# B times delta u by token on GpSimd, in four more states of a selective scan

## The reference

```python
# u: (b, 128, 256), four directions k; delta = softplus(...); A = -exp(A_logs); 16 states n
def step(h, inp):
    dt, bt, ct, ut = inp
    h = exp(dt[..., None] * A) * h + (dt * ut)[..., None] * bt[:, None, :]
    return (h, einsum('bdn,bn->bd', h, ct))
ys = vmap(_selective_scan)(xs, delta, A, Bst, Cst, Ds)      # k = 0..3
y = ys.sum(0); y = (y * silu(z)) @ out_proj_w
```

## Time and profile before

| what | us |
|---|---|
| median of three runs | 206.13 |
| profiled execution | 204.65 |
| its span | 202.9 |
| scans, first start to end of the last | 20.55 to 115.2 |
| busy in the span: PE, DVE, ACT, POOL | 191.7, 156.7, 140.0, 96.3 |
| granted TensorE clock | 1.000 |

### The profile page before, as it was taken

One profiled execution on the slowest core, in us unless ns is written; L12 is line 12 of the kernel. 1 busy time (PEld: TensorE's weight loads), 2 busy tenths in 40 slices (PEclk: granted clock), 3 DMA queues, 4 the chain that ended last, 5 costly groups with the idle time before them and its releaser, 6 DMA issues.

```text
span 202.9 us, 2710 instructions
## 1 busy us (share of the span) xinstructions
PE 191.7 (94%) x784; PEld 88.0 (43%) x784; DVE 156.7 (77%) x264; ACT 140.0 (69%) x292; POOL 96.3 (47%) x117
## 2 busy tenths in 40 slices
PE   7799999799999978999999999989999999999992
PEld 2334654344545434455355457664323333333331
DVE  6386899999999999999999864857376664663843
ACT  3529896999999999989999814547836255253431
POOL 7575668698899859998899700000000000000000
PEclk9999999999999999999999999999999999999999
DMA  4799554438967679793956000000000000000000
GB/s 133 158 240 167 139 183 110 145 131 205 231 235 197 177 205 270 220 222 132 304 221 218 15 0 0 3 0 0 0 3 0 2 2 0 0 3 0 0 0 26
DMA packets 17661, 21.79 MB, mean 107 GB/s; under 512 B 7721, under 2 KB 9198, under 8 KB 17646
## 3 DMA queue, kind: packets, MB, share of 16 engines
q1 hardware_dynamic: 17470, 21.52, 38.1%
q10 hardware_dynamic: 176, 0.10, 0.2%
HBM read 21.35 MB, written 0.26 MB: 107 GB/s over the span
## 4 chain that ended last, share of the span: by engine, by line
PE 48%; DMA 12%; DVE 8%; POOL 6%; issue 5%; SPq 0%; DVEq 0%; ACT 0%; POOLq 0%
PE ps L1177 20%; PE ps L1192 11%; DMA cr<-c_rows 9%; PE ps L965 8%; POOL rings L411 6%; DVE rings L692 4%; DMA c_rows<-cb 3%; PE ps L972 2%; PE ps L888 1%; DVE ps L682 1%; PE ps L1199 1%; PE ps L1133 1%; PE ps L1152 1%; PE ps L1053 1%; PE ps L1104 1%
## 5 line engine op out<-in xcount | busy, mean ns | idle before, releaser
L411 POOL TENSOR_TENSOR rings<-rings,cr 128x512 f32<-128x512 f32 x59 | 73.3, 1275 | 10.3 <-DVE rings L692 4.7
L692 DVE TENSOR_TENSOR_SCAN rings<-rings,ps 128x512 f32<-128x512 f32 x64 | 74.4, 1203 | 0.8 <-ACT rings L502 0.4
L859 DVE TENSOR_TENSOR rings<-ps,si 128x512 f32<-128x512 f32 (+1 forms) x44 | 30.4, 691 | 25.3 <-ACT si L584 24.4
L584 ACT ACTIVATE si<-ps 128x512 f32<-128x512 f32 (+1 forms) x44 | 26.3, 597 | 32.7 <-PE ps L1177 32.5
L502 ACT ACTIVATE rings<-delta,a_neg 128x510 f32<-128x510 f32 x64 | 43.5, 707 | 0.1
L1177 PE MATMUL ps<-fd,wup 64*128 64x512 f32 (+1 forms) x176 | 41.5, 607 | 0.6 <-DVE fd L794 0.5
L483 ACT ACTIVATE scaled<-du_tok,b_tok 128x128 f32<-128x128 f32 x116 | 36.7, 387 | 0.4 <-PE ps L972 0.3
L965 PE MATMUL ps<-rings,ident 128*128 128x512 f32 x64 | 33.1, 598 | 1.9 <-POOL rings L411 1.9
L965 PE MATMUL ps<-rings,flip 128*128 128x512 f32 x64 | 32.3, 598 | 0.4 <-POOL rings L411 0.4
L1177 PEld LDWEIGHTS ps<-fd,wup 64*128 64x128 f32 (+1 forms) x176 | 15.9, 182 | 24.5 <-issue 14.1
L682 DVE TENSOR_TENSOR ps<-ps,du 128x512 f32<-128x512 f32 x35 | 23.5, 679 | 1.6 <-PE ps L991 1.0
(11 more groups left out here) (211 smaller groups left out, 171.9 us busy)
## 6 DMA issues: line engine op xcount, KB each, us to landing
cr<-c_rows SPq DMA_DIRECT2D x60, 256.0 KB, 3.9
wup<-w_up_dram SPq DMA_DIRECT2D x8, 341.0 KB, 5.8
wdn<-w_down_dram SPq DMA_DIRECT2D x4, 160.0 KB
wdn<-w_down_dram SPq DMA_DIRECT2D x4, 128.0 KB
w_conv<-conv_w_dram SPq DMA_DIRECT2D x1, 384.0 KB, 5.5
xc<-x_chan_dram SPq DMA_DIRECT2D x2, 128.0 KB, 4.7
w_conv<-conv_w_dram SPq DMA_DIRECT2D x1, 192.0 KB, 4.5
xg<-x_grp_dram SPq DMA_DIRECT2D x1, 128.0 KB, 2.8
```

The source lines that it names most:

```text
L411: nc.gpsimd.tensor_tensor(hc[:, q], hs[:, q], cr[:, row_slot(n)] if n >= ROWS_FROM else cs[:, q], ALU.mult).then_inc(weighted, 1)
L584: nc.scalar.activation(si[0:rows, S % 2, :], ps[0:rows, BANK_H + 2 * (S % 3), :], ACT.Silu).then_inc(silu_ready, 1)
L692: nc.vector.tensor_tensor_scan(hs[:, q, :], da[:, q].rearrange("p b l -> p (b l)"), driven(q), 0.0, ALU.mult, ALU.add).then_inc(scanned, 1)
L859: nc.vector.tensor_tensor(gated[0:rows, S % GATED, :], ps[0:rows, BANK_H + 2 * (S % 3) + 1, :], si[0:rows, S % 2, :], ALU.mult).then_inc(g ...
```

## The change

Four states more, 8, 10, 25 and 41, have the driving term made by token. Their product of delta u and B is one POOL instruction (a tensor product of 128x512, B's value repeated over 128 channels) into a buffer `scaled_p` of its own, six states ahead of its use; PE turns it into the bank with four transposes, in place of the one spreading matmul, and DVE's product for that state goes away. The four products share one buffer, so each waits until PE has turned the one before it (`b_ready`).

```diff
 SCALE_LEAD = 2
+POOL_SCALED = [8, 10, N + 9, 2 * N + 9]
+POOL_LEAD = 6
+BY_TOKEN = sorted(SCALED + POOL_SCALED)
...
+        scaled_p = sb("scaled_p", [P, NT, D])
...
+            def scale_state(n):
+
+                j, k = POOL_SCALED.index(n), n // N
+                pool.wait_ge(bt_kept, 1)
+                pool.wait_ge(dut_kept, k + 1)
+                if j:
+                    pool.wait_ge(b_ready, POOL_SCALED[j - 1] + 1)
+                col = k % 2 * N + n % N
+                nc.gpsimd.tensor_tensor(scaled_p[:], du_tok[:, k % 2], b_tok[:, :, k // 2, col:col + 1].broadcast_to([P, NT, D]),
+                                        ALU.mult).then_inc(pool_scaled, 1)
...
                     if n in TIMES_AT:
                         times_u(k + 1)
+                    if n + POOL_LEAD in POOL_SCALED:
+                        scale_state(n + POOL_LEAD)
...
-                    if n in SCALED:
+                    if n in BY_TOKEN:
                         return
...
             def turn_scaled(n):
-                j = SCALED.index(n)
-                pe.wait_ge(scaled_ready, j + 1)
+                if n in POOL_SCALED:
+                    pe.wait_ge(pool_scaled, POOL_SCALED.index(n) + 1)
+                    tiles = scaled_p[:]
+                else:
+                    j = SCALED.index(n)
+                    pe.wait_ge(scaled_ready, j + 1)
+                    tiles = scaled[:, j % 2]
                 for t in range(NT):
-                    last = nc.tensor.transpose(driven(n % BODY)[:, t * P:(t + 1) * P], scaled[:, j % 2, t, :], ident[:])
+                    last = nc.tensor.transpose(driven(n % BODY)[:, t * P:(t + 1) * P], tiles[:, t, :], ident[:])
                 last.then_inc(b_ready, 1)
...
-                        if n in SCALED:
+                        if n in BY_TOKEN:
                             turn_scaled(n)
                         else:
                             spread_b(k, n)
```

More of the change, by code:

```diff
@@ L210, in hybrid_kernel @@
             sem(n) for n in ("bt_ready", "bt_kept", "dut_ready", "dut_kept", "scaled_ready"))
+        pool_scaled = sem("pool_scaled")
         rows_kept, rows_out = sem("rows_kept"), sem("rows_out")
@@ L686, in scan @@
                     dve.wait_ge(da_ready, n + 1)
-                    if n in SCALED:
+                    if n in BY_TOKEN:
                         dve.wait_ge(b_ready, n + 1)
                     else:
-                        dve.wait_ge(b_used, n + 1 - sum(m < n for m in SCALED))
+                        dve.wait_ge(b_used, n + 1 - sum(m < n for m in BY_TOKEN))
                     wait(dve, weighted, n - BODY + 1)
```

## The result

The changed kernel takes 1.008 times as long as the kernel before (95% interval 1.0058 to 1.0101), some 1.6 us more; the medians of twenty runs of each are 205.54 and 205.26 us. One sentence is needed to read these numbers: in part of the executions of either kernel the work ahead of the scans takes up to some 4 us longer, the ratio leaves the slowest executions out, and the three runs of before that the forecast started from (206.13 us) lie in the upper half of the twenty.

The account below looks back on a forecast made before the run. The bound was taken as GpSimd's back-to-back weightings and the queue and DMA of C's rows up to state 48, then fixed PE work. 206.13 + 2 x 1.235 (states 25 and 41) = 208.6 us, range 207.0 to 209.9.

Parts of the forecast that it names:

- The way to the end: GpSimd's back-to-back states 19 to 25 and 32 to 41, C's two row writes, state 48, then 19.3 us of PE.
- its lead: VectorE's scan of state 39 waits for a weighting at 81.10, read as VectorE being the full four states ahead.
- The products on GpSimd: Each new 128x512 product on GpSimd was priced at the weighting's 1.235 us, with 1.03 and 2.5 as ends.
- the sum: Terms of states 25 and 41 added over the whole kernel: 2 x 1.235 = +2.47 us, all other terms 0.
- States 25 and 41 on the way, 8 and 10 not: Products of 25 and 41 in GpSimd's back-to-back runs cost +1.235 us each; those of 8 and 10 cost 0.
- the stall at state 10: GpSimd waits for PE before state 10's product; expected made up, term 0; rival that it stays, up to +1.0 us, chance 0.05.
- The write moves with the weighting that it stands behind: On SP's queue, C's row writes of directions 2 and 3 come later with states 25 and 41, 1.235 us per product.
- VectorE gains nothing: VectorE's four dropped products, 0.59 us a step at state 25, only lengthen its lead or precede other waits; no gain.
- the transposes cost nothing: On PE, turning instead of spreading adds 0.25 us in each of four states, covered by idle time or waits; term 0.
- VectorE as the bound: Rival: VectorE sets the end of the scans, so four steps of 0.59 go, 2.36 us, median 203.8; chance 0.12.
- the DMA way swallows a delay: Rival: C's row writes issued later land as early as before; one delay lost 207.4, chance 0.10, both 206.1, chance 0.08.
- the difference of 1.48 us: Whole kernel: the median of the runs lies 1.48 us above the profiled execution; the same distance was assumed after the change.

Follow-up runs that it names:

- products made and not used: Changed kernel with the four GpSimd products still made but unused, the four states spread and multiplied on VectorE as before; ratio 1.0049 to the kernel before.
- state 37: Kernel before with state 37 alone by token on GpSimd, its product behind state 31 where GpSimd waits for a row, late write; ratio 0.9982.

## Why the prediction was right or wrong

**The way to the end.** The step that failed is the sentence "So the end of the scans is the time at which state 48 is weighted, plus fixed PE work". It holds for the profiled execution of before and for every profile of the changed kernel with the late write, but not for the two other executions of before, where the write was 1.0 and 1.3 us shorter and VectorE set the end at 99.16 us. The wait of VectorE for GpSimd that the prediction read as its lead (0.21 us at 81.10) isn't there in those two either. I took one execution's way to the end for the kernel's. The gap of 1.29 us ahead of state 48 told nothing about that; what would have was the length of a write of 32 KB, 7.0 us in one place and 5.1 in the other.

**The products on GpSimd.** 1.235 us was the step of the nearest row; the new product steps 1.00 to 1.01. It went past the low end that I had kept (1.03). Two on the way make 2.0, not 2.47. That this much arrives at state 48 is shown by two profiles with writes of the same length, states 8 and 10 alone against 25 and 41 alone: 79.56 - 77.53 = 2.03 us. At `yg` only 100.22 - 99.16 = 1.06 us is left, because the first 0.97 us brings state 48 from 77.53 up to the 78.5 where it starts to count. With a long write in before, all of the 2.0 counts. The measured 1.6 us lies between. This is the loss: two products of 1.0 us, less the room that a short write leaves. Of the 0.87 us too much in the sum, 0.46 is the price of the two products; the other 0.4 fits that room, which the prediction put at nothing.

**States 25 and 41 on the way, 8 and 10 not.** Right. The two late products make the whole loss, the two early ones none that can be told with the late write, and the stall at state 10 (2.54 us) is made up at state 16.

**The write moves with the weighting that it stands behind.** Right, and shown by taking it away: with the write issued early, the changed kernel goes from 1.008 to 0.9957 against the kernel before, while the kernel before itself goes to 0.9975, which can't be told from no change. The run with states 25 and 41 alone and the early write doesn't confirm it by its times, only by its profile.

**VectorE gains nothing.** Wrong for the kernel before, right for the changed one. Leaving its four products out gave 0.9 us; where the write is out of the way, the two late products take `yg` from 99.16 to 98.55, half of their two steps of 0.59. With the late write none of that is seen.

**TensorE.** That the transposes cost nothing can't be told from the times: products made and not used cost 1.0 us, the whole change 1.6, with intervals that overlap. The profiles bear it out. Without the transposes (products unused) state 25 is weighted at 47.26, from state 32 to the next write it is 14.95 us, and from state 48 to `yg` 20.67; in the second profile of the changed kernel the same pieces are 47.29, 14.96 and 20.67. What differs between the two are the writes.

**The rivals.** VectorE as the bound was half true: it is the floor under the kernel before, 0.95 us below the profile that I had. The rival in which the DMA way swallows a delay named the right place with the wrong reason: the write doesn't land at the same time when issued later. Issued 1.0 us later it took 6.0 us in the mean of four profiles, against 5.9 in seven; what it does is vary, by 1.6 us over these eleven. Neither had the form "two ways to the end that are within 1 us of each other", which is what it was.

**The level.** I carried the difference of 1.48 us between three runs and the profile over to the result. Those three lay 0.87 us above the median of twenty, and together with the 0.87 us too much in the sum this is enough to put the time below the range. The other 1.3 us between 208.6 and 205.54 is the difference between the 1.6 us of the ratio and the 0.28 us between the two medians. In the fourteen profiles the first delta-u product begins between 16.61 and 21.03 us, in kernels that are the same up to there, and it follows the time at which TensorE's clock rises (last section). An estimate from the profiles: 206.13 us less the stretch of 99.16, the 85.2 behind it and the 1.7 between a profiled run's time and its span is a start of 20.1 us, one of the long ones.

## What to carry to other kernels

Before an engine's idle time is used as a measure of what an added instruction costs, look at how far the next way to the end lies behind; a wait that a DMA ends may be of another length in the next execution, so one profile shows one of the two ways and not both. A queue that mixes a rarely needed write with loads that wait for other engines makes that write inherit their delays: issuing it four row loads earlier took the loss of this change away. An instruction for an engine off the critical path goes where that engine waits (state 37, behind state 31), not where it runs back to back.

## What the runs showed of the hardware

A GpSimd product of 128x512 with one operand that repeats each of four values 128 times took 1046 ns in the mean, against 1277 for a product of two full operands in the same kernel (line, engine, operation, operands, count | busy us, mean ns):

```profile
L427 POOL TENSOR_TENSOR rings<-rings,cr 128x512 f32<-128x512 f32 x59 | 73.3, 1277 | 4.4 <-DVE rings L710 2.5 <-DMA cr<-c_rows 1.8
L413 POOL TENSOR_TENSOR scaled_p<-du_tok,b_tok 128x512 f32<-128x512 f32 x4 | 4.2, 1046 | 2.5 <-PE ps L995 2.5
```

That is the time of the one-input copy of 512 columns in the earlier trace rows, 1050 ns. The Trainium skill ("GPSIMD Engine Reference", section "Performance versus the Vector engine") puts the cost of a two-input product down to two operands that take turns at one read port. A repeated operand that costs like one input would fit that, though no run here shows the port itself. The price per small read command, which the prediction weighed, is not seen.

The same six convolution matmuls ahead of the scans took 2.84 us in the profile of the kernel before and 4.41 us in that of the changed one (start, us, engine, line). Before:

```profile
9.86 2.84 PE L928 MATMUL ps<-x_col,w_fold 128*128 128x512 f32 x6
```

After:

```profile
10.78 4.41 PE L946 MATMUL ps<-x_col,w_fold 128*128 128x512 f32 x6
```

TensorE's clock is the difference. In the profile with state 41 alone they took 5.31 us, and there the record of the clock covers them (the stretches as above, the clock is the third number from the right):

```profile
5.50:8.90 3.40, 2.11 (x13) 0.99 (x14) 0.63 (x3) 1.54 (x3) 1.07 (x8) 1.00 0.83 185
9.00:15.80 6.80, 6.80 (x12) 2.35 (x8) 5.73 (x18) 1.83 (x4) 5.04 (x24) 0.50 0.89 205
15.80:20.00 4.20, 4.20 (x12) 1.64 (x12) 0.65 (x3) 1.73 (x2) 1.00 (x1) 1.00 0.96 166
...
10.80 5.31 PE L946 MATMUL ps<-x_col,w_fold 128*128 128x512 f32 x6
```

A granted clock of 1.00 is the upper of its two levels, 2.4 GHz, and 0.50 the lower, 1.2 GHz. PE was busy 2.11 of the 3.40 us ahead of the fall, and all of the 6.80 us ahead of the rise. These matmuls begin 0.85 us apart at 0.50, and 0.43 us apart in the kernel before. In the profile of the changed kernel the table of stretches prints 1.00 for this time, but its trace has no record of the clock ahead of 13.96 us; up to there the matmuls begin 0.85 to 0.86 us apart, behind it 0.44. So they ran at the lower level there too.

The start of the scans follows this. The record of the upper level that lasts through the scans begins at 4.1 to 5.9 us in six profiles, and the first delta-u product at 16.61 to 17.62; at 9.7 to 10.2 in three, and 18.06 to 18.26; at 13.9 to 14.0 in three, and 20.08 to 20.16; at 15.4 and 15.8 in two, and 20.65 and 21.03. What sets the time of the rise was not tried.
